# One VectorE operation for causal mask, negation and row maximum in a two-layer attention kernel

## The reference

```python
scores = jnp.einsum('bhqd,bhkd->bhqk', q, k) * scale
causal = jnp.tril(jnp.ones((s, s), dtype=bool))
scores = jnp.where(causal, scores, jnp.asarray(-1000000000.0, scores.dtype))
attn = jax.nn.softmax(scores, axis=-1)
out = jnp.einsum('bhqk,bhkd->bhqd', attn, v)
out = out.transpose(0, 2, 1, 3).reshape(b, s, H * D)
return out @ Wo.T
```

## Time and profile before

| what | value |
|---|---|
| median of the runs | 2505.04 us (2501.7 to 2507.02, 3 runs) |
| the profiled execution's span | 2500.1 us |
| PE busy | 2252.5 us, 90% of the span |
| DVE busy | 1672.9 us, 67% |
| ACT busy | 1045.2 us, 42% |
| POOL busy | 1013.6 us, 41% |
| DVE row maxima, L1506, 512 of them | 388.1 us |
| DVE mask additions, L1504, 512 of them | 148.6 us |

### The profile page before, as it was taken

How to read it: one execution, slowest core, us unless ns; L and a number is a source line. 1 busy time by engine, 2 the same in 40 slices (tenths; PEclk the granted TensorE clock), 3 DMA queues, 4 the chain that set the end, 5 groups by cost and what they waited for, 6 DMA issues and landing times. The chain is left out here.

```text
span 2500.1 us, 34935 instructions
## 1 busy us (share of the span) xinstructions
PE 2252.5 (90%) x11154; PEld 1811.5 (72%) x11154; DVE 1672.9 (67%) x3685; ACT 1045.2 (42%) x2182; POOL 1013.6 (41%) x1036
## 2 busy tenths in 40 slices
PE   5767359899999999999999796999999999999998
PEld 4623147688888878888877684788788888888886
DVE  4299966476767667676767455667676767666765
ACT  4323213344444445454544232444454544454443
POOL 2655251264545536363644100435262524343341
PEclk9879679999999999999999898999999999999999
DMA  9500045501010110101010434201101010101010
GB/s 337 185 9 1 1 183 200 180 10 64 8 64 23 50 36 37 56 18 56 23 48 1 163 133 179 85 26 42 50 17 50 25 59 8 59 8 59 20 35 30
DMA packets 74002, 164.82 MB, mean 66 GB/s; under 512 B 4704, under 2 KB 38880, under 8 KB 67296
## 3 DMA queue, kind: packets, MB, share of 16 engines
q1 hardware_dynamic: 73504, 162.69, 18.6%
q10 hardware_dynamic: 432, 1.32, 0.1%
HBM read 113.14 MB, written 72.61 MB: 74 GB/s over the span
## 5 line engine op out<-in xcount | busy, mean ns | idle before, releaser
L1472 POOL TENSOR_TENSOR probs<-probs,rinv 128x1024 f32<-128x1024 f32 (+7 forms) x384 | 439.7, 1149 | 1020.7 <-DVE rinv L1511 1020.5
L1554 ACT ACTIVATE probs<-psum,nmax 128x256 f32<-128x256 f32 (+7 forms) x512 | 381.6, 745 | 498.4 <-DVE nmax L1506 497.2
L1520 DVE TENSOR_TENSOR pT<-psum,pT 128x512 fp32r<-128x512 f32 x576 | 386.2, 687 | 233.4 <-ACT pT L1560 233.3
L1560 ACT ACTIVATE pT<-psum 128x512 fp32r<-128x512 f32 x576 | 329.7, 597 | 271.7 <-PE psum L1613 269.3
L1506 DVE TENSOR_REDUCE nmax<-psum 128x1 f32<-128x256 f32 (+7 forms) x512 | 388.1, 758 | 17.5
L1613 PE MATMUL psum<-ident,probs 128*128 128x128 f32 x2304 | 330.8, 274 | 19.2 <-issue 11.3
L1613 PEld LDWEIGHTS psum<-ident,probs 128*128 128x128 f32 x2304 | 272.4, 140 | 72.0 <-DVE pT L1520 18.3
L93 PE MATMUL psum<-pT,vals 128*128 128x512 f32 x576 | 258.7, 449 | 19.9 <-DVE pT L1520 17.6
L93 PE MATMUL psum<-keys,q 128*128 128x512 f32 (+3 forms) x768 | 265.7, 346 | 5.3 <-DVE q L1493 2.8
L95 PE MATMUL psum<-keys,q 128*128 128x512 f32 (+3 forms) x768 | 261.9, 341 | 0.0
L94 PE MATMUL psum<-keys,q 128*128 128x512 f32 (+3 forms) x768 | 261.8, 341 | 0.0
(11 more groups left out here) (266 smaller groups left out, 3931.0 us busy)
## 6 DMA issues: line engine op xcount, KB each, us to landing
k_parts<-kv_out SPq DMA_DIRECT2D x32, 512.0 KB, 4.9
wq<-wq_copy SPq DMA_DIRECT2D x16, 1024.0 KB, 4.8
wo<-wo_copy SPq DMA_DIRECT2D x16, 1024.0 KB, 4.9
v_parts<-kv_out SPq DMA_DIRECT2D x32, 512.0 KB, 4.0
keys<-k_parts SPq DMA_DIRECT2D x32, 512.0 KB, 4.7
vals<-v_parts SPq DMA_DIRECT2D x64, 256.0 KB, 3.2
acc<-in_x SPq DMA_DIRECT2D x4, 1024.0 KB, 11.9
xn_later<-xn SPq DMA_DIRECT2D x1, 2048.0 KB, 14.0
```

The costliest lines, as they stand in the source:

```text
L1472: pool.tensor_tensor(p, p, rinv[:, u, h:h + 1].to_broadcast([P, (TB - u) * P]), ALU.mult).then_inc(p_ok, 1)
L1520: dve.tensor_tensor(pT[:, n % PT_SLOTS, 1, :], bank[T_BANK + n % 2], f32(pT[:, n % PT_SLOTS, 0, :]), ALU.subtract).then_inc(t_lo, 1)
L1554: act.activation(probs[:, u % 2, h, 0:n], bank2[2 * (h % 2)][:, off:off + n], ACT.Exp, bias=nmax[:, u, h:h + 1], accum_out=rsum[:, u, h:h ...
L1560: act.activation(pT[:, n % PT_SLOTS, 0, :], bank[T_BANK + n % 2], ACT.Copy).then_inc(t_hi, 1)
```

## The change

One VectorE instruction over the whole row takes the place of two. `tensor_tensor_reduce` computes out = (in0 + in1) x (-1) and a running minimum over out, begun at 2e30. in0 and out are the score row in PSUM, n columns wide; in1 is the last n columns of a new tile `causal` in bfloat16, zero but for the triangle in its last 128 columns; the minimum of the negated row is the negated maximum, and goes to `nmax`. So PSUM holds the negated scores afterwards, and the exponential reads them with scale -1. The wait for the scores now stands on a semaphore increment of its own ahead of the instruction (`sem_inc` on `s_seen`, for which nobody waits). `causal` is made by POOL at the start of each of the two attentions, and DVE waits for it once, before the passes. `m.mask` and its making at the program's start go. `probs` becomes two tiles, of which the odd one is 896 columns wide.

```diff
             pool.memset(m.ident[:], 0.0).then_inc(const, 1)
-            pool.memset(m.mask[:], 0.0).then_inc(const, 1)
...
-            pool.affine_select(out=m.mask[:], in_=m.mask[:], compare_op=ALU.is_ge, fill=MASKED,
                                base=0, pattern=[[-1, P]], channel_multiplier=1).then_inc(const, 1)
...
-        probs = sb("probs", [P, 2, REP, S])
+        probs = [sb("probs_even", [P, REP, S]), sb("probs_odd", [P, REP, S - P])]
+        causal = sb("causal", [P, S], BF16)
...
         def _(pool):
 
+            pool.memset(causal[:], 0.0).then_inc(causal_ok, 1)
+            pool.wait_ge(causal_ok, 1)
+            pool.affine_select(out=causal[:, S - P:S], in_=causal[:, S - P:S], compare_op=ALU.is_ge, fill=MASKED,
+                               base=0, pattern=[[-1, P]], channel_multiplier=1).then_inc(causal_ok, 1)
...
                         dve.wait_ge(s_mm, it * SC + (REP * u + h + 1))
-                        diagonal = bank2[2 * (h % 2)][:, off + n - P:off + n]
-                        dve.tensor_tensor(diagonal, diagonal, m.mask[:], ALU.add).then_inc(s_masked, 1)
-                        dve.wait_ge(s_masked, it * SC + (REP * u + h + 1))
-                        dve.tensor_reduce(nmax[:, u, h:h + 1], bank2[2 * (h % 2)][:, off:off + n], AX.X, ALU.max,
-                                          negate=True).then_inc(s_max, 1)
+                        dve.sem_inc(s_seen, 1)
+                        row = bank2[2 * (h % 2)][:, off:off + n]
+                        dve.tensor_tensor_reduce(out=row, in0=row, in1=causal[:, S - n:S], scale=-1.0, scalar=-2 * MASKED, op0=ALU.add,
+                                                 op1=ALU.min, accum_out=nmax[:, u, h:h + 1]).then_inc(s_max, 1)
...
             for k in range(REP):
                 query_low(REP + k, k + 1, True)
+            dve.wait_ge(causal_ok, 2)
             with dve.Fori(0, ITERS - 1) as it:
...
-                        act.activation(probs[:, u % 2, h, 0:n], bank2[2 * (h % 2)][:, off:off + n], ACT.Exp,
+                        act.activation(probs[u % 2][:, h, 0:n], bank2[2 * (h % 2)][:, off:off + n], ACT.Exp, scale=-1.0,
                                        bias=nmax[:, u, h:h + 1], accum_out=rsum[:, u, h:h + 1]).then_inc(p_exp, 1)
```

More of the change, by code:

```diff
@@ L173, in _ @@
             pool.memset(mhalf[:], -0.5).then_inc(const, 1)
-            pool.wait_ge(const, 5)
+            pool.wait_ge(const, 4)
             pool.affine_select(out=m.ident[:], in_=m.ident[:], compare_op=ALU.not_equal, fill=1.0,
-                               base=0, pattern=[[-1, P]], channel_multiplier=1).then_inc(const, 1)
-            pool.affine_select(out=m.mask[:], in_=m.mask[:], compare_op=ALU.is_ge, fill=MASKED,
                                base=0, pattern=[[-1, P]], channel_multiplier=1).then_inc(const, 1)
@@ L306, in _ @@
         def _(pe):
-            pe.wait_ge(const, 7)
+            pe.wait_ge(const, 5)
             def turn_x(n):
@@ L1222, in layer1_attention @@
         o_hi, o_lo, w_mm, x_add = (sem("e_" + n) for n in ("o_hi", "o_lo", "w_mm", "x_add"))
-        stored, s_masked = sem("e_stored"), sem("e_s_masked")
+        stored, causal_ok, s_seen = sem("e_stored"), sem("e_causal"), sem("e_s_seen")
         mixes_later = b < B - 1
@@ L1469, in body @@
                         u, h = arg
-                        p = probs[:, u % 2, h, 0:(TB - u) * P]
+                        p = probs[u % 2][:, h, 0:(TB - u) * P]
                         pool.wait_ge(p_inv, it * SC + (REP * u + h + 1))
@@ L1612, in body @@
                         for h in range(REP):
-                            ins = pe.transpose(bank[T_BANK + n % 2][:, h * P:(h + 1) * P], probs[:, u % 2, h, j * P:(j + 1) * P], m.ident[:])
+                            ins = pe.transpose(bank[T_BANK + n % 2][:, h * P:(h + 1) * P], probs[u % 2][:, h, j * P:(j + 1) * P], m.ident[:])
                         ins.then_inc(t_mm, 1)
@@ L1666, in program @@
         m.ident, m.ones, m.zero = consts("ident", [P, P]), consts("ones", [P, P]), consts("zero", [P, 1])
-        m.mask = consts("mask", [P, P])
         kept = Column(nc, KEPT, 207.8)
```

## The result

| | before | after |
|---|---|---|
| median of the runs, us | 2503.61 (2501.7 to 2507.02, 4 runs) | 2465.71 (2463.85 to 2468.43, 4 runs) |
| profiled execution: its time, its span, us | 2505.04, 2500.1 | 2463.85, 2461.6 |
| mean granted clock over the span | 0.961 | 0.962 |

It is faster, so the sign was right; the size was not.

What follows compares the result with a forecast made beforehand. PE's matmuls were taken to bind, with PE waiting on late DVE. 14 x 5.6 x 0.254 = 19.9 us plus 2 x 8.0 x 0.254 = 4.1 us, less 2 us, made 22 us: 2483 us, range 2468 to 2503.

Steps and rivals of the forecast that it cites:

- What bounds the kernel: Both attentions: PE's matmuls bind, busy 112.9 to 113.2 of 115 us; only PE's waits for late DVE can shrink.
- What goes: DVE, per head: the mask addition L1504, 290 ns, and the 0.03 us hop to the maximum go, together 0.324 us.
- The main part at the maximum's own duration: DVE: the new instruction's main part takes as long as the old maximum L1506 over n columns, so no change.
- The two steps a column: Rival, DVE: new instruction costs 1.04 ns a column more, +33 us, 2530 to 2550; chance 0.10, shared with longer POOL waits.
- the hold beside GpSimd: Rival: POOL holds the new DVE instruction up by 0.26 us, saving gone, 2500 to 2510; chance 0.10, shared with no effect.
- The readout: DVE, per head: reading out the minimum adds about 0.07 us, between nothing and 0.23, leaving 0.254 us saved.
- the free readout: Case where DVE's readout of the minimum costs nothing: 94 x 0.324 = 30 us gained, time down to 2468; chance 0.04.
- The wait on its own: DVE's separate wait for the scores adds a 0.11 us hop 32 times, at most 3.5 us; 1 us counted.
- The number of places: Chain of waits: L1504's share gives 5.6 places in each of 14 passes and 8.0 in each of 2 last passes, 94.
- What is late next: Next limits: ACT's high part ready 0.43 us early, transposes idle 0.40 us; 1 us taken off for shorter stalls.
- The last passes: Last pass of each attention: 8.0 places x 0.254 us, about 2 us each, 4.1 us for both.
- The range: Whole kernel: 2468 to 2503 us, leaving out the slow cases and most without effect, 0.16 to 0.18.

Runs made afterwards that it cites:

- two_ops: Changed kernel with the mask addition, semaphore and negated maximum put back in place of the fused instruction, all other edits kept; 2507.37 us, ratio 1.0012.
- f32_mask: Changed kernel with the second attention's mask tile in fp32, the first's still bfloat16; 2464.98 us, ratio 0.9846.

## Why the prediction was off

**What bounds the kernel: right.** PE, waiting for the low part behind a maximum. Busy PE stayed the same work, the waits went.

**What goes, 0.324 us a head: right.** DVE's queue shows 0.33 (below).

**The main part at the maximum's own duration: right,** 9 ns too low. The two steps a column (2538 us) and the hold beside GpSimd fell: 767 ns on the mean, 284 to 1233.

**The readout, 0.07 us: half right.** It is an instruction of its own, as the Trainium skill has it (VectorE: DVE Perf Modes, section Two Vector instructions with no wait between them). The page gives no duration; here it takes 141 ns, like the 155 ns row chosen for it. But it costs two different things. For ACT: from the start of head 3's first instruction to the exponential, 1.31 us became 1.04 (749.71 to 751.02, 750.18 to 751.22), 0.27 saved. For DVE's queue the next instruction starts with the readout at 751.04, so it costs nothing: 0.33 saved. So it is in 207 of the 512 places of the changed kernel, where the next instruction starts at most 10 ns behind the readout. The forecast had 0.254 for both, and gave the free readout a chance of 0.04.

**The wait on its own: counted at 1 us, not seen.** DVE idles for the scores 48 times instead of 32, 33.3 us instead of 26.8, but two_ops, which has that wait too with all the other edits, stands at the kernel before's time at equal clock.

**The number of places: the step that failed.** 5.6 places a pass x 0.254 us = 1.42 us; measured 1.99 in the second attention and 2.29 in the first. At the prices just read, 0.27 to 0.33, the pass of the second attention holds the worth of 6.0 to 7.4 places, that of the first of 6.9 to 8.5, and not of 5.6. The price was too low as well, by 6 to 30%, but even at 0.33 the 5.6 places make 1.85 us.

What the count missed can be read from the kernel before. The 5.6 came from a share of time divided by 0.290 us. The chain's own pieces have L1504 six times in that pass, in lengths of 0.21 to 0.31 us, and eleven times, not 8.0, in the stretch with the last pass. And two kinds of place aren't among them. The first are stalls shorter than the overlap of two matmuls:

```profile
1774.99 0.29 DVE L1504 TENSOR_TENSOR psum<-psum,mask 128x128 f32<-128x128 f32 x1
...
1775.79 0.68 DVE L1520 TENSOR_TENSOR pT<-psum,pT 128x512 fp32r<-128x512 f32 x1
...
1776.53 0.51 PE L93 MATMUL psum<-pT,vals 128*128 128x512 f32 x1
```

Addition and maximum stand ahead of the low part, and L93 starts 0.34 us behind L95 (1776.19) instead of 0.23; at 1787.89 it is the same with the accumulation L1528 in place of L1520. The chain counts this time as PE's L93 (0.44 us from 1776.59) and has no DVE in it. The prediction says of PE's waits that such gaps don't show, and didn't carry that over to the chain. The changed kernel gains 0.49 of its 1.97 us a pass at these two places. The second kind goes through an exponential. At the first long stall the addition of head 2 runs at 1733.08, its exponential from 1734.40 to 1735.30 and the turn's high part behind that, but the chain has only

```profile
1734.62 0.58 issue
```

within the exponential, and leads on to ACT's wait for the turn's transposes; the addition isn't on it. Fusing head 2 alone took 0.20 us off this stall. "issue" can thus be a busy engine: 0.82 us of it at 1736.95 are DVE in L1506 (1736.90 to 1737.86).

Not every place counted gave its saving either. The transposes of the earlier trace rows stood for 0.40 us and stand for 0.35 in the changed kernel (1692.52), so 0.05 us of the saving passed through there; and two of the six pieces, at 1795.73 and 1796.27, belong to a stall whose gain of 0.33 us is lost again at the matmuls behind it. So 5.6 was too low on balance, by errors both ways.

The first attention was set equal to the second because its busy times were, and was 0.3 us a pass better. Most of that is one place, where PE's transposes wait for DVE's multiplication of the fourth head, L1516. In the first attention it takes 1.35 us there (802.66) beside POOL's L1457 of the mixing, which runs from 802.58 for 1.28 us, and in the same place of the second 0.35 us (1790.42). It ends at 804.01 and PE's transposes start at 804.11, after 0.31 us of idleness; with the change they come 0.32 us earlier against the matmuls ahead of them.

**What is late next: right as a mechanism, too cautious as a place.** The loop of transposes and copies is next, with 0.25 us left at both long stalls. The forecast's cut-off was the 0.43 us of slack of a single instruction; two savings of 0.27 and 0.33 fell into one stall of 0.64 and 0.39 us of them came through; of the same two at the stall of 0.78, 0.53. The other reading of it failed: in the earlier trace rows the saving was to pass through to the transposes, up to 0.40 us, and 0.05 did.

**The last passes.** 2 us each: right in the second attention (2.1) and in the pair with the mixing moved away (2.2). The 8 us of the profiled pair hold a clock that no row of the kernel before could have given to the change. With the 3 us of clock in the medians left out, the miss is 34 against 22.

**The range.** Its low end, 2468, took the price of a place to its bound (0.324) and left their number at 94. With 14 x 7.5 + 2 x 8 = 121 places, the 7.5 taken from the result, the gain is 33 to 40 us at 0.27 to 0.33; with the 14 x 6 + 2 x 11 = 106 pieces that the chain had before the change, 27 at the forecast's price and 34 at its bound. The number had been read from a single share and was the weaker of the two factors; it should have had bounds of its own.

## What to carry to other kernels

An instruction of an in-order engine that feeds another engine has two prices, when its result arrives and how long it keeps its own queue, and where two of them lie in one path both are collected at the same stall. Before multiplying a saving by places on the chain, look through which engine each stall reaches the bound, and give the number of places a range: the chain names only the last link, its "issue" can be time in which an engine was at work, and a stall shorter than the overlap of two matmuls isn't on it. Count its pieces rather than dividing its share, and look at the distances between the starts of the matmuls. Applying a change to a part of its places (here by head) tells in one run which of them matter.

## What the runs showed of the hardware

- A readout of DVE's accumulator takes 141 ns, and the instruction behind it can start together with it (751.04 and 751.04; at most 10 ns behind in 207 of 512 places): there it costs the queue nothing measurable.
- The instruction with two sources, one in PSUM, that writes back to PSUM and keeps a minimum took as long as a plain reduction of its width, with a mask of either type: 284 ns at its shortest, 1233 at its longest.
- A stand of PE of 2.2 us was followed by a granted clock of 0.57 over the next 4 us in one execution of the same instructions (f32_mask) and by 1.00 in another (the changed kernel).
- DVE's L1517 from SBUF to SBUF, 128x384, took 1.45 us beside POOL's L1459 in the last pass of the first attention, and 0.42 in the same place of the second, where POOL doesn't mix:

```profile
1351.29 1.26 POOL L1459 TENSOR_TENSOR acc<-acc,product 128x512 f32<-128x512 f32 x1
1351.32 1.45 DVE L1517 TENSOR_SCALAR probs_odd<-probs_odd,rinv 128x384 f32<-128x384 f32 x1
...
2430.79 0.42 DVE L1517 TENSOR_SCALAR probs_odd<-probs_odd,rinv 128x384 f32<-128x384 f32 x1
```
